# A two-layer transformer on one core: head groups written out, keys awaited by piece, the causal diagonal cleared on GpSimd, feed-forward normalisation on ScalarE

## What is computed

```python
x = L0_attn_x                                      # (1, 4096, 256)
x = _layernorm(x + _L0_attn_ref(x, ...))           # 16 heads, causal
x = _layernorm(x + _L0_ffn_ref(x, ...))            # fp4-rounded gate, up, down; width 704
x = _layernorm(x + _L1_attn_ref(x, ...))           # 16 heads, every key
x = _layernorm(x + _L1_ffn_ref(x, ...))            # coupling nets, three cycles
# in both attentions
scores = einsum('bhqd,bhkd->bhqk', q, k) / 4       # layer 0: where(causal, scores, -inf)
out = einsum('bhqk,bhkd->bhqd', softmax(scores), v)
```

## Time and profile before

| | us |
|---|---|
| median of 3 runs | 5524.33 |
| lowest and highest | 5508.73, 5526.52 |
| the profiled execution | 5519.82 |
| its span | 5518.0 |
| PE, DVE, ACT, POOL busy in it | 5035.9, 4698.1, 3736.7, 213.0 |

### The profile page before, as it was taken

How to read it: one execution, slowest core, us unless ns; L and a number is a source line. 1 busy time by engine, 2 the same in 40 slices (tenths; PEclk the granted TensorE clock), 3 DMA queues, 4 the chain that set the end, 5 groups by cost and what they waited for, 6 DMA issues and landing times. The chain is left out here.

```text
span 5518.0 us, 124529 instructions
## 1 busy us (share of the span) xinstructions
PE 5035.9 (91%) x43370; PEld 2086.1 (38%) x43370; DVE 4698.1 (85%) x5343; ACT 3736.7 (68%) x7102; POOL 213.0 (4%) x262
## 2 busy tenths in 40 slices
PE   7589999999999578875999999999999999999777
PEld 4233434433434245542333333333333333333333
DVE  3588879789889689847999999999999999999835
ACT  2068778687787311131888888888888888888523
POOL 3100000000000000030000000000000000000200
PEclk7589999999999789995999999999999999999988
DMA  4301010010010000051100001000100001000000
GB/s 126 102 17 32 11 28 21 14 39 11 11 41 10 24 14 11 5 192 39 39 7 8 5 5 42 8 5 5 27 23 5 5 8 42 5 8 5 4 9 27
DMA packets 152676, 143.01 MB, mean 26 GB/s; under 512 B 72234, under 2 KB 106986, under 8 KB 152042
## 3 DMA queue, kind: packets, MB, share of 16 engines
q1 hardware_dynamic: 152074, 134.93, 8.7%
HBM read 86.84 MB, written 46.66 MB: 24 GB/s over the span
## 5 line engine op out<-in xcount | busy, mean ns | idle before, releaser
L926 DVE TENSOR_REDUCE att_mx<-ps 128x2 f32<-128x1024 f32 (+2 forms) x3335 | 3897.2, 1192 | 288.1 <-PE ps L801 211.1
L907 ACT ACTIVATE att_probs<-ps 128x512 f32<-128x512 f32 (+3 forms) x6400 | 3390.3, 583 | 643.2 <-PE ps L843 198.3
L870 PE MATMUL ps<-att_probs,att_V 128*17 128x256 f32 (+1 forms) x25088 | 1950.7, 385 | 0.0
L843 PE MATMUL ps<-att_Q,K 50*128 50x512 f32 (+3 forms) x6400 | 1676.9, 491 | 42.1 <-ACT att_probs L907 23.3
L801 PE MATMUL ps<-K,att_Q 48*128 48x512 f32 x6670 | 1458.7, 418 | 140.7 <-DMA K<-khi_scratch 82.1
L843 PEld LDWEIGHTS ps<-att_Q,K 50*128 50x128 f32 x6400 | 649.9, 185 | 1384.0 <-ACT att_probs L907 1314.6
L870 PEld LDWEIGHTS ps<-att_probs,att_V 128*17 128x17 f32 x25088 | 424.9, 95 | 1054.9 <-issue 591.7
L801 PEld LDWEIGHTS ps<-K,att_Q 48*128 48x128 f32 x6670 | 667.6, 192 | 230.0 <-DVE att_mx L926 138.0
L887 ACT ACTIVATE att_negT<-ps 32x128 fp32r<-32x128 f32 x66 | 16.6, 251 | 232.3 <-PE ps L811 232.3
L1181 PE MATMUL ps<-wguT,mlp_xqT 128*128 128x512 f32 (+1 forms) x384 | 166.1, 584 | 0.3 <-DVE mlp_h L1284 0.2
L791 PE MATMUL ps<-att_band,att_pick 64*128 64x128 bf16 x2080 | 162.6, 223 | 0.0
(11 more groups left out here) (211 smaller groups left out, 2391.3 us busy)
## 6 DMA issues: line engine op xcount, KB each, us to landing
K<-khi_scratch SPq DMA_DIRECT2D x320, 64.0 KB, 2.3
att_Q<-qhi_scratch SPq DMA_DIRECT2D x272, 64.0 KB, 2.3
att_V<-v_scratch SPq DMA_DIRECT2D x80, 136.0 KB, 2.5
K<-klo_scratch SPq DMA_DIRECT2D x160, 64.0 KB, 2.3
v_scratch<-proj_vpad SPq DMA_DIRECT2D x16, 544.0 KB, 3.4
att_Q<-qlo_scratch SPq DMA_DIRECT2D x136, 64.0 KB, 2.3
att_Q<-att_negT SPq DMA_DIRECT2D x264, 4.0 KB
proj_x<-in_L_attn_x SPq DMA_DIRECT2D x8, 512.0 KB, 5.2
```

The source lines that it names most:

```text
L843: mm = pe.matmul(ring(at)[:, lo:QB], K[rows, u // NQB, j, kt * P:(kt + 1) * P], Q[rows, slot_of(u), j, lo:QB], start=True, stop=not diagonal)
L870: mm = pe.matmul(ps[VW * h:VW * h + HV, 6, lo:(part + 1) * (QB // 2)], V[:, v // NQB, kt, HV * h:HV * (h + 1)], probs[:, (n_key[v] + kt) % ...
L907: act.activation(probs[:, (n_key[u] + kt) % PBUFS, column(h), lo:QB], ring(at)[:, lo:QB], ACT.Exp, scale=SCALE).then_inc(emptied, 1)
L926: dve.tensor_reduce(mx[:, min(u % NQB, 1), :, j, qt, c], ps[:, 2 + 2 * pair:4 + 2 * pair, 0:max_width(u, i) // 2], AX.X, ALU.max).then_inc ...
```

## The change

In attention `UNITS` becomes 32, all four groups, and the loops over `gp` are gone. No index is taken modulo `UNITS` any more: the last unit hosts nothing, SP loads nothing for a pass that doesn't follow, and there is no blank step. Waits against `gp * per_ring + ...` become waits against constants. Unit 16 follows unit 15 as any other unit follows.

The first group's key pieces get a semaphore each (`k_first`), and PE waits for a piece at the first maximum that reads it.

In layer 0 the scores are no longer banded; the maxima still are. After the exponentials of a diagonal key tile POOL clears, in place, the part of the masked square above the diagonal in `probs`, four heads in one `affine_select` of 128 partitions by 4 x 128. PE's value matmuls of these tiles wait for POOL (`masked`) instead of ACT (`emptied`). That is 128 selects.

In `mlp`, DVE's `norm` goes. POOL makes `shift` = -mean x rstd after the power, as a second small operation behind a wait, and ACT applies scale and shift (`apply`) at the end of its list for the iteration, behind the Silu. ACT's and POOL's loops there are written out.

```diff
--- before.py
+++ after.py
     pre = f"att{layer}_"
-    UNITS = 2 * NQB
+    GROUPS = HEADS // GH
+    UNITS = GROUPS * NQB
...
+    ahead = [0 if u + 2 >= UNITS or causal and u % NQB >= NQB - EARLY else
+             round(len(maxima(u + 2)) * SEAM / (keys(u) * GH)) for u in range(UNITS)]
+    before = 0 if causal else round(len(maxima(1)) * SEAM / (NT * GH))
+    hosted = [[(u + 1, i) for i in range(ahead[u - 1] if u else before, len(maxima(u + 1)))
+               if u + 1 < UNITS and ((u + 1) % NQB or not causal)] +
+              [(u + 2, i) for i in range(ahead[u])] for u in range(UNITS)]
...
-    for first in (0, NQB) if causal else ():
-        hosts = [(first - EARLY + e) % UNITS for e in range(EARLY)]
+    for first in range(NQB, UNITS, NQB) if causal else ():
+        hosts = range(first - EARLY, first)
...
-        if u == UNITS - 1:
-            while (at_ring + sum(step[0] in RING for step in plan[u])) % 3:
-                plan[u].append(("blank",))
...
+                    pool.wait_ge(ones_set, 10)
+                    for u in range(UNITS):
+                        for kt in range(keys(u) - QT, keys(u)):
+                            pool.wait_ge(emptied, last_score(u, kt) + 4)
+                            square = probs[:, (n_key[u] + kt) % PBUFS, :, width(u, kt):width(u, kt) + P]
+                            pool.affine_select(out=square, in_=square, compare_op=ALU.is_ge, fill=0.0, base=0,
+                                               pattern=[[0, GH], [1, P]], channel_multiplier=-1).then_inc(masked, 1)
...
-                load_queries(0, 0)
+                load_queries(0)
                 for piece in range(NQB):
-                    load_keys(0, 0, piece)
-                load_queries(0, 1)
+                    load_keys(0, piece, k_first[piece])
+                load_queries(1)
                 place_max(-1, 0)
...
+                for u in range(UNITS):
+                    group = u // NQB
+                    if u:
+                        sp.wait_ge(scored, n_ring[u] + 1)
+                    more = u % NQB == 1 and group + 1 < GROUPS
+                    if more:
+
+                        sp.wait_ge(values_done, n_key[u] + PBUFS)
+                        load_queries((group + 1) * NQB)
...
+                    if u + 2 < UNITS and (u + 2) % NQB:
+                        load_queries(u + 2)
+                    if more:
+                        for piece in range(NQB):
+                            at = place[u][plan[u].index(("score", LAG + 2 + 3 * piece, 0))]
+                            sp.wait_ge(scored, at + 2)
+                            load_keys(group + 1, piece, k_got[(group + 1) % 2])
+                    if u + 1 < UNITS:
                         i = [step[0] for step in plan[u]].index("turn_max")
-                        place_max(gp * per_ring + place[u][i], (u + 1) % UNITS)
-                for u in range(4):
-                    sp.wait_ge(q_got[slot_of(u)], 96 * (2 * loads_per_pass(u) + (1 if u < 2 else 0)))
-                for par in range(2):
-                    sp.wait_ge(max_got[par], 64 * (UNITS + (1 if par == 0 else 0)))
-                sp.wait_ge(k_got[0], 3 * K_LANDED)
-                sp.wait_ge(v_got[0], 3 * V_LANDED)
+                        place_max(place[u][i], u + 1)
...
-                pe.wait_ge(k_got[0], K_LANDED)
+                    pe.wait_ge(ones_set, 10)
                 pe.wait_ge(q_got[slot_of(0)], 96)
                 for n, (w, i) in enumerate(before_loop):
                     if n == len(maxima(0)):
                         pe.wait_ge(q_got[slot_of(1)], 96)
+                    elif w == 0 and (i == 0 or maxima(0)[i][2] != maxima(0)[i - 1][2]):
+                        pe.wait_ge(k_first[maxima(0)[i][2]], 96)
...
-                with pe.Fori(0, 2) as gp:
-                    for u in range(UNITS):
-                        now = gp * UNITS + u
-                        nk = keys(u)
-
-                        pe.wait_ge(max_got[u % 2], gp * (64 * UNITS // 2) + 64 * (u // 2 + 1))
...
-                                mm = pe.matmul(ring(at)[:, lo:QB], K[rows, u // NQB, j, kt * P:(kt + 1) * P],
-                                               Q[rows, slot_of(u), j, lo:QB], start=True, stop=not diagonal)
-                                if diagonal:
-                                    for m in range(2):
-                                        mm = add_band(ring(at)[:, lo:lo + P], b, 1, m)
-                                mm.then_inc(scored, 1)
...
-                                if part == 0:
-                                    last = place[v][plan[v].index(("score", kt, GH - 1))]
-                                    pe.wait_ge(emptied, gp * per_ring + last + 4)
...
+                            mm = pe.matmul(ring(at)[:, lo:QB], K[rows, par_of(u), j, kt * P:(kt + 1) * P],
+                                           Q[rows, slot_of(u), j, lo:QB], start=True, stop=True)
+                            mm.then_inc(scored, 1)
...
+                            if part == 0:
+                                if causal and kt >= keys(v) - QT:
+                                    pe.wait_ge(masked, v * QT + kt - (keys(v) - QT) + 1)
+                                else:
+                                    pe.wait_ge(emptied, last_score(v, kt) + 4)
...
-                pipeline(act, NT, [(7, keep_h), (0, keep_o), (4, keep_x), (5, silu)])
+
+                def apply(n):
+                    def step(j, par):
+                        done(act, s[f"root{n + 1}"], j)
+                        act.activation(o_all[:, j, :], y[n][:], ACT.Identity, bias=shift[n][:, 0:1], scale=rstd[n][:, 0:1]
+                                       ).then_inc(s[f"x{n + 1}_made"], 1)
+                    return step
+                pipeline(act, NT, [(7, keep_h), (0, keep_o), (4, keep_x), (5, silu), (2, apply(0)), (9, apply(1))], unroll=True)
...
-                        pool.tensor_tensor(rstd[n][:], var[n][:], power[:], ALU.pow).then_inc(s[f"root{n + 1}"], 1)
+                        pool.tensor_tensor(rstd[n][:], var[n][:], power[:], ALU.pow).then_inc(s[f"scale{n + 1}"], 1)
+                        pool.wait_ge(s[f"scale{n + 1}"], j + 1)
+                        pool.tensor_scalar(shift[n][:], mv[n][:, 0:1], rstd[n][:, 0:1], -1.0, ALU.mult, ALU.mult
+                                           ).then_inc(s[f"root{n + 1}"], 1)
                     return step
-                pipeline(pool, NT, [(9, root(1)), (2, root(0))])
+                pipeline(pool, NT, [(9, root(1)), (2, root(0))], unroll=True)
...
-                def norm(n, j):
-                    done(dve, s[f"root{n + 1}"], j)
-                    dve.tensor_scalar(tile(j), y[n][:], mv[n][:, 0:1], rstd[n][:, 0:1],
-                                      ALU.subtract, ALU.mult).then_inc(s[f"x{n + 1}_made"], 1)
...
-                    if second is not None:
-                        norm(1, second)
-                    if first is not None:
-                        norm(0, first)
```

More of the change, by code:

```diff
@@ L575, in attention @@
             given = upto
-    before_loop = [(0, i) for i in range(len(maxima(0)))] + [(1, i) for i in range(ahead[-1])]
+    before_loop = [(0, i) for i in range(len(maxima(0)))] + [(1, i) for i in range(before)]
     max_number, n_max = {}, len(before_loop)
@@ L634, in loads_before, with par_of @@
         return sum(slot_of(v) == slot_of(u) for v in range(u))
[L636 to L637 removed]
+    def par_of(u):
+        return u // NQB % 2
     def width(u, kt):
@@ L787, in _, with add_band @@
             @block.tensor
             def _(pe):
-                def add_band(dst, b, kind, m):
+                def add_band(dst, b, m):
                     rows = slice(b * HALF, (b + 1) * HALF)
-                    return pe.matmul(dst, pick[rows, m], band[rows, m, kind], start=False, stop=(m == 1))
+                    return pe.matmul(dst, pick[rows, m], band[rows, m], start=False, stop=(m == 1))
                 def take_max(i, u, at, pair):
@@ L801, in take_max @@
                         mm = pe.matmul(bank(b)[:, 0:wide], Q[rows, slot_of(u), j, qt * P:(qt + 1) * P],
-                                       K[rows, u // NQB, j, c * QB:c * QB + wide], start=True, stop=not diagonal)
+                                       K[rows, par_of(u), j, c * QB:c * QB + wide], start=True, stop=not diagonal)
                     if diagonal:
```

239 lines of the change are left out of this document (104 added, 135 removed).

## The result

| | us |
|---|---|
| before, median of 4 runs in the same comparison | 5521.51 |
| after, median of 4 runs (5447.85 to 5458.25) | 5455.32 |
| ratio, with its 95% interval | 0.9882 (0.9861 to 0.9902) |
| span of the profiled execution after | 5452.2 |

The change gains 66 us, 1.2%. The forecast was a gain of 156 and 5363.6 us, and the range ended at 5405. The direction was right. The size was wrong by more than half.

What follows compares the result with a forecast made beforehand. The prediction took TensorE's order to bound the attention steps and VectorE the feed-forward. Its terms (46.8 + 17.3 + 18 + 7.9 + 2 + 38 - 0.8 + 27 = 156.2) taken from 5519.8 gave 5363.6 us, range 5320 to 5405.

Steps and rivals of the forecast that it cites:

- Key waits: Start of both attentions: waiting per key piece lets TensorE start at about 206.1 instead of 229.48, 23.4 us each, 46.8 in all.
- TensorE's own order sets the step: Second attention loop, steady state: TensorE's instruction order sets the 1.22 us step, VectorE 0.09 behind, ScalarE's two exponentials within 0.98.
- a steady step other than 1.22: Attention loops in the changed profile: a step time the prediction listed as showing it wrong.
- rival (d): Attention loops: register work was part of the 1.22 us step, which falls to 1.13; about 5085 us, chance 0.05.
- 1.22 - 0.98 = 0.24: Last attention units: each removed useless maximum saves 0.24 us, the difference between steps with and without one.
- terms 17.3 and 18: Useless maxima removed: layer 1 gains 17.0 plus 0.3 for gather and turn, layer 0 gains 18 (15 to 21).
- Seam: Between the two attention passes: no pipeline emptying or loop jump, gaining 7.9 us in layer 1, 2 in layer 0.
- Band, 38 us: Layer 0 diagonal: band matmuls leave the scores, GpSimd's select (taken as 1.0 us) stays hidden; gain 38 us (20 to 48).
- Feed-forward, 27 us: Feed-forward stage: normalisation moved to ScalarE cuts iterations from 11.9 to 10.9 us, gaining 27 us (8 to 33).
- (a): Layer 0 diagonal: selects at 2.18 us overrun their cover, costing 38 us; 5402 us, chance 0.09.
- (b): Layer 0 diagonal: selects become the bound, all gains eaten from 3.5 us each; 5630 us at 4.36, chance 0.04.
- (c): Feed-forward gives nothing, as ScalarE sits behind Silu and TensorE's 10.7 us bound next; 5390 us, chance 0.13.

## Why the prediction went wrong

**Key waits: right.** 23.4 foreseen in each layer; -26.3 and -23.0 in the stages, the first maxima at 203.29 instead of 229.48. Of the 26.2 in layer 0, 2.8 lie ahead of the attention: its first query transfer is issued at 195.61 instead of 198.38.

**Steady step, the sentence "TensorE's own order sets the step": right as far as it went, and the step that failed.** TensorE does set 1.22 us, as the short exponentials and the reordered waits show. But the sentence gave ScalarE all the room between 0.98 and 1.22, and the loop through the ring has so little room that 0.06 us before one exponential in four used it up. In the changed kernel the step is 1.233 us, and "a steady step other than 1.22" stood among the prediction's own signs of being wrong. I read throughput (two exponentials fit) where latency counts (score end, exponential, bank free, next score). And the part on "waits against constants" was costed at nothing, or as a gain in rival (d). I never asked which of two waits the instruction would carry once both became constants. It cost 28 us in layer 1 and about 13 in undisturbed layer 0.

**Price of a maximum, "1.22 - 0.98 = 0.24": wrong by a factor of two.** The earlier trace rows showed one step without a maximum among steps with one, and that is short. A row of them isn't. Changed kernel, last unit of layer 1:

```profile
5050.54 0.50 PE L839 MATMUL ps<-att_Q,K 50*128 50x512 f32 x2
...
5051.52 0.76 PE L839 MATMUL ps<-att_Q,K 50*128 50x512 f32 x2
...
5052.77 0.50 PE L839 MATMUL ps<-att_Q,K 50*128 50x512 f32 x2
...
5053.76 0.75 PE L839 MATMUL ps<-att_Q,K 50*128 50x512 f32 x2
```

0.98, 1.25, 0.99: the steps alternate, 1.11 on the mean of a pair. The unit took 72.3 us and not 64 (70.4 with the waits reordered, where the steps alternate between 0.98 and 1.18). So a removed maximum was worth 0.11 us there, 0.14 with the waits reordered. In the last group of layer 0, units at full clock with and without them (26: 60.83 and 59.81 us, 28: 42.13 and 41.65, 29: 32.19 and 30.82, 30: 21.73 and 20.03, with the waits reordered in all, 3 us at the lower clock in the 41.65; 46 maxima) give 0.10. Of the terms 17.3 and 18 some 8 to 10 and 6 were real.

**Seam: right** in layer 1 (167.3 us for units 15 and 16 before, 161.4 after, 159.8 with the waits reordered). The 2 us of layer 0 are too few to be told from what the clock does there.

**Band, 38 us: mechanism and size right, the sum wrong.** The select took 0.635 us, under the 1.0 taken and inside the bounds, no idle time of TensorE stands against it, and the inner diagonals fell from 10.23 to 8.97 us. That is 1.26 us, more than the "at most 1.1" of the prediction, so at full clock the term is 45 us and not 38 (its 0.19 a step should read 0.20, too). What the term left out is the clock. By the rule of the Trainium skill that the prediction weighed ("GPSIMD Engine Reference", 3.1 Elementwise) the select would have been some 5.1 us, an estimate, if it counts as such branching; the measurement decides against its use here.

**The clock: absent from the prediction.** Every gain was worked out at the clock of the rows, 0.98 to 1.00. The attention loop of layer 0, from its first exponential to its last unit, spent 75 us at the lower level before and 179 after (added up from the changes of the granted clock in the trace; the table of stretches gives the same size); at 0.38 each these 104 us are 40. They, 13 for the wait and 12 of the 18 for maxima make 65, less the 7 that the band gained more, and 61 are missing in layer 0. In layer 1 the wait (28) and the term for maxima (9) make 37, and 38 are missing. That the sums close so well is in part luck, for the price of 0.38 comes from one unit and the time at the lower level in the first three groups differs by some 50 us between kernels whose code there is the same. The Trainium skill ("TensorE: Matmul & The Clock Gate", HAM oscillation) describes kernels whose clock falls in waits for transfers and stays low for the next piece of work. The last group here has such a wait (0.93 us in unit 27), and the clock is at its lower level in the work behind it, so the trace agrees so far; but filling the wait was not enough, and filling the thin steps was.

**Feed-forward, 27 us: right in size, not in the iteration.** An iteration takes 11.07 us (transposes of `h` at 2055.63 and 2066.70), not 10.9. Before, iterations of 11.9 were mixed with some of 12.7 and 12.9 at a lower clock (0.92 over the stage), which the change removed too (0.97). One table load in the stage, as foreseen.

**Rivals.** None gave 5455. The range's lower end, 5320, rests on "30 down", where the bounds of the terms give 22; it played no part. (a) and (b) fell with the select's 0.635 us, (c) with 380 us, and (d) with the short exponentials: without register work the step is still 1.22. The missing rival was "thinner work lowers the clock", for which the trace of the kernel before had a sign: 9 to 14 us at half clock in the first unit of each of layer 0's groups, three of them behind the short units that end a group.

**What stays open.** What the useless matmuls are worth in the whole time beside the reordered waits, since the intervals overlap; why the lower clock comes in one unit rather than another in the first three groups; and how much the reordered waits gain in the last group by the clock (0.81 to 0.92) and how much by the step. What sets the step once TensorE has less to do, the loop or VectorE, is open too.

## What to carry to other kernels

When a change takes work away from TensorE in a stretch that isn't saturated, look at the granted clock of that stretch first and put a price on a fall (here 0.38 us for each microsecond at the lower level); useless matmuls in the thin place can be cheaper than none (here 220 us for 246 in six units). When an instruction waits for two things, see in the instruction list which wait it carries, and let it be the one that arrives last. Price a removed operation from a run of steps without it and not from a single one: the neighbours of a single one fill the pipeline for it.

## What was unexpected of the hardware

- A wait in a semaphore instruction of its own delayed the exponential by 0.06 us (0.096 after the score's end in place of 0.037), and reordering the waits gave 52 us of 5455.
- Some 160 matmuls whose results nobody reads made the last six units of layer 0 take 220 us and not 246 (granted clock 0.98 for 0.80 in the stretch around them).
- GpSimd's select over 128 partitions by 512 elements took 0.635 us on the mean of 128, little more than twice the 0.29 us of one with 128 elements.
